# Slot numbers of a routed expert layer found for two experts at a time, in four rounds

## The chip, the cores and the metric

The kernel is one program on one core of a Trainium2 chip. The core has five engines that run their own instruction streams and meet only at semaphores: TensorE (PE, matrix products; its weight loads are listed apart as PEld), VectorE (DVE), ScalarE (ACT), GpSimd (POOL) and SyncE (SP, which issues most DMA transfers). The metric is the device time of one execution in microseconds. Smaller is better.

## What is computed

A decoder block on `x` of 2 x 1024 tokens by 256: a linear recurrence with a gate, a cross attention of 16 heads, and an expert layer, each followed by a sum with its input and a layer norm. The change lies in the expert layer, whose reference is, cut to what matters:

```python
Sm = jax.nn.softmax(xf @ Wr + br, axis=-1)     # 2048 tokens, 8 experts
G_t, idx_t = jax.lax.top_k(Sm.T, k)            # each expert takes its k = 256 tokens
tokens = xf[idx]
mid = jax.nn.silu(jnp.einsum('keh,ehf->kef', tokens, W_up[group]) + b_up[group])
out = jnp.einsum('kef,efh->keh', mid, W_down) + b_down
y = jnp.zeros_like(xf).at[idx].add(G[..., None] * out)
```

## The kernel before

Everything is written out by hand: no scheduler moves an instruction, and each engine runs its rows in the order of the code. Eight PSUM banks are handed out by a table (`product(name, bank)`): PE takes its turn on a bank with `turn(name)`, which waits until the last result there was moved away, and `wait_filled` and `wait_moved` are the waits of the others.

The expert layer begins with 15 rounds of a search for each expert's threshold (DVE and ACT count, PE adds up). Then DVE turns the chosen tokens into slot numbers 0 to 255 for each expert: prefix sums, two products for the offsets (banks 4 and 5), and the slot split in a high and a low digit of 16 values each, `sl_f` (L1960). What follows is what the change touches, the way from slots to `idx`, the token number of each slot:

- DVE compares both digits with 0 to 15 for all eight experts at once (`one_hot`, L1966). A one-hot tile is 128 partitions by 16 columns of tokens (NT) by 16 digit values by 8 experts. This is done in two halves over NT: low digit `OHL`, high digit `OHH`, then `OHT` = `OHL` times the token number (L1975). ACT spread the token numbers over `token_b` in two parts beside rounds 10 and 11 of the search (L1057).
- PE adds 16 products of `OHH` and `OHT` up in bank 6 (L1500, product "ids"). It gives 128 x 128 numbers: (high digit, expert) by (low digit, expert), of which those of the same expert count.
- DVE masks them (`ym`), sums over experts (`lk`) and multiplies by a mask of row positions (`lh`): L1980, L1983, L1984. PE makes one product with `mask_16` (L1505, "idx"), and DVE copies it out as whole numbers (`idx`, L1987).
- POOL then issues 16 indirect DMAs (L832), one for 128 rows of `XG` each. Gathers 2e and 2e+1 are the tokens of expert e. PE meanwhile makes 12 products that nobody reads (`keep_busy(0, 12)`, L1154).

Then `expert_steps` runs: "gt" transposes an expert's tokens (PE L1514 and L1520; ACT copies them to `FTH`, DVE makes the low part `FTL`), "up" is three pairs of products into banks 0, 1, 2, 7 in turn (L1544 for the first six, then L1144), with SiLU in place and `MH` by ACT (L1088, L1094 to L1097) and `ML` by DVE (L2007 to L2011), "dn" is the product with `W_down` (L1564), scaled by DVE (`OUT`, L1997) and added to DRAM by POOL (L842). Expert 0 is gt 0, up 0 and 1, gt 1, up 2. POOL issues no L842 before the sixteenth gather.

## Time and profile before

| | us |
|---|---|
| median of three runs | 317.17 |
| lowest and highest | 316.96, 317.83 |
| the profiled execution | 318.26 |
| its span | 316.1 |
| PE busy | 254.3 (80%) |
| DVE busy | 199.7 (63%) |
| ACT busy | 156.0 (49%) |
| POOL busy | 133.8 (42%) |

The span is the time from the first to the last instruction of the profiled execution. 2.16 us of that execution lie around it. The rows further down are from this execution, in microseconds from its span's start. The stretch from `sl_f` to the end of expert 0 is about 200 to 236 us. A row of the timeline gives an operation's start and length, the engine and the line, what is written and read, and in brackets how long the engine had been idle before it and what ended that. The chain of waits is followed back from the last instruction of the program, so that each piece of it is a piece of the time.

### The profile page before, as it was taken

To read this page: it belongs to the slowest core of one execution; us is meant where nothing else is said; L and a number is where in the kernel's file an instruction comes from. 1 tells how busy PE (TensorE), PEld (TensorE's weight loads), DVE (VectorE), ACT (ScalarE), POOL (GpSimd) and SP (SyncE) were. 2 spreads that over 40 slices of the span, in tenths; PEclk is the share of its full clock that TensorE was granted. 3 is DMA by queue.
4 is the path that set the end of the run, shared out by engine and by line. 5 is a ranking of instruction groups with operands and counts; after the bars stand their busy time and mean duration, and the time that the engine had idled before them with its cause. 6 is when DMAs were issued, how large, how long until landed. Compare 5 with 4: busy or idle time off the path is not lost.

```text
span 316.1 us, 5069 instructions
## 1 busy us (share of the span) xinstructions
PE 254.3 (80%) x1647; PEld 204.6 (65%) x1647; DVE 199.7 (63%) x613; ACT 156.0 (49%) x322; POOL 133.8 (42%) x211
## 2 busy tenths in 40 slices
PE   8989999899898999999963111385679999999791
PEld 4744557575556789988951101245679999999790
DVE  1744467378867578578785998810156676777394
ACT  4643312534778364744232775102147787875224
POOL 6817915525353135543232491067521333333133
PEclk9999999999999999999995555569569999999998
DMA  6960031045385638200004999123303856422646
GB/s 188 305 108 1 1 76 27 0 89 110 70 181 99 154 70 181 50 2 3 1 0 112 318 408 350 53 68 107 101 0 45 229 125 137 115 29 27 155 149 261
DMA packets 33403, 35.59 MB, mean 113 GB/s; under 512 B 10338, under 2 KB 25698, under 8 KB 33122
## 3 DMA queue, kind: packets, MB, share of 16 engines
q1 hardware_dynamic: 30002, 31.16, 35.6%
q0 software_dynamic: 2784, 4.00, 7.5%
q8 instruction: 14, 0.23, 0.3%
q10 hardware_dynamic: 592, 0.12, 0.2%
q14 instruction: 11, 0.09, 0.1%
HBM read 18.16 MB, written 8.19 MB: 83 GB/s over the span
## 4 chain that ended last, share of the span: by engine, by line
PE 56%; DVE 18%; ACT 10%; issue 4%; POOL 4%; another core or an unknown queue 4%; DMA 3%; SPq 0%; DVEq 0%; POOLq 0%; ACTq 0%
PE bank L1144 11%; PE bank L1381 8%; PE bank L1564 6%; PE bank L1332 4%; PE bank L1230 3%; DVE junk L1905 3%; PE bank L1154 3%; PE bank L1301 2%; PE bank L1368 2%; ACT bank L1088 2%; POOL rstd L778 2%; PE bank L1315 2%; DMA Y<-summed_rows 2%; PE bank L1404 1%
## 5 line engine op out<-in xcount | busy, mean ns | idle before, releaser
L777 POOL TENSOR_SCALAR var_eps<-mean_var 128x1 f32<-128x1 f32 (+2 forms) x37 | 8.4, 228 | 79.7 <-DVE mean_var L1752 79.2
L842 POOL DMA_INDIRECT summed_rows<-OUT,idx x14 | 21.7, 1550 | 44.9 <-DVE OUT L1997 42.8
L1381 PEld LDWEIGHTS bank<-VB,PT 128*128 128x128 f32 x256 | 32.4, 191 | 1.5
L1144 PE MATMUL bank<-FTH,WUH 128*128 128x256 f32 x94 | 28.0, 298 | 6.3 <-issue 6.3
L1381 PE MATMUL bank<-VB,PT 128*128 128x34 f32 x256 | 30.9, 268 | 0.0
L1088 ACT ACTIVATE bank<-bank,b_up_c 128x256 f32<-128x256 f32 (+1 forms) x48 | 19.5, 446 | 22.3 <-remote 11.0
L1564 PE MATMUL bank<-WDH,MH 128*128 128x256 f32 x80 | 24.3, 303 | 3.6 <-DVE ML L2011 3.2
L1144 PE MATMUL bank<-FTL,WUH 128*128 128x256 f32 x94 | 27.1, 289 | 0.0
L1144 PE MATMUL bank<-FTH,WUL 128*128 128x256 f32 x94 | 27.1, 288 | 0.0
L1759 DVE TENSOR_REDUCE NMF<-bank 128x8 f32<-128x512 f32 x32 | 21.7, 680 | 6.6 <-PE bank L1344 6.3
L2007 DVE TENSOR_TENSOR ML<-bank,MH 128x512 fp32r<-128x512 f32 x16 | 11.0, 688 | 20.7 <-ACT MH L1094 20.7
L778 POOL TENSOR_TENSOR rstd<-var_eps,neg_half 128x1 f32<-128x1 f32 (+2 forms) x37 | 22.7, 615 | 3.1
L832 POOL DMA_INDIRECT XG<-routed_rows,idx x16 | 15.5, 966 | 20.3 <-DVE idx L1987 15.7
L1564 PE MATMUL bank<-WDH,ML 128*128 128x256 f32 x80 | 23.4, 292 | 0.1
L1564 PE MATMUL bank<-WDL,MH 128*128 128x256 f32 x80 | 23.4, 292 | 0.0
L1144 PEld LDWEIGHTS bank<-FTH,WUH 128*128 128x128 f32 x94 | 18.8, 200 | 6.5 <-issue 6.5
L953 ACT ACTIVATE PT<-bank 128x512 f32<-128x512 f32 x32 | 18.6, 596 | 6.0 <-PE bank L1368 5.9
L1564 PEld LDWEIGHTS bank<-WDH,MH 128*128 128x128 f32 x80 | 16.1, 201 | 4.4 <-DVE ML L2011 4.0
L1144 PEld LDWEIGHTS bank<-FTL,WUH 128*128 128x128 f32 x94 | 18.9, 201 | 0.0
L1144 PEld LDWEIGHTS bank<-FTH,WUL 128*128 128x128 f32 x94 | 18.7, 199 | 0.0
L1477 PE MATMUL bank<-cnt,same_expert 128*128 128x3 bf16 x15 | 2.5, 164 | 19.4 <-DVE junk L1905 19.4
L1368 PE MATMUL bank<-QS,KS 128*128 128x512 f32 x32 | 15.2, 474 | 2.9 <-ACT QS L988 1.3
(341 smaller groups left out, 761.6 us busy)
## 6 DMA issues: line engine op xcount, KB each, us to landing
WDR<-in_L_ffn_W_down SPq DMA_DIRECT2D x8, 640.0 KB
QS<-QH SPq DMA_DIRECT2D x32, 128.0 KB, 2.6
WUR<-in_L_ffn_W_up SPq DMA_DIRECT2D x4, 682.0 KB, 5.4
routed_rows<-X SPq DMA_DIRECT2D x2, 1056.0 KB, 10.3
X<-in_x SPq DMA_DIRECT2D x4, 512.0 KB, 5.2
QS<-QL SPq DMA_DIRECT2D x16, 128.0 KB, 2.6
summed_rows<-X SPq DMA_DIRECT2D x2, 1024.0 KB, 9.7
Y<-summed_rows SPq DMA_DIRECT2D x8, 256.0 KB, 5.0
```

Of the source, the lines that this page charges most:

```text
L778: pool.tensor_tensor(rstd[:, at], var_eps[:, at], neg_half[:, 0:width], ALU.pow).then_inc(ln_pool, 1)
L832: pool.indirect_dma_start(XG[:, s, :], None, routed, bass.IndirectOffsetOnAxis(ap=idx[:, s:s + 1].bitcast(U32), axis=0)).then_inc(gathered ...
L842: pool.indirect_dma_start(summed, bass.IndirectOffsetOnAxis(ap=idx[:, 2 * e + h:2 * e + h + 1].bitcast(U32), axis=0), OUT[:, (2 * e + h) % ...
L953: act.activation(PT[m % 2][:, j, :], bank_of(("sc", m, j))[:], ACT.Exp, scale=SCALE)\
L1088: last = act.activation(mid[0:w, i], mid[0:w, i], ACT.Silu, bias=b_up_c[0:w, g, f:f + 1])
L1144: last = pe.matmul(o, a, b, start=(n == 0), stop=(n == 3 * len(pairs) - 1))
L1332: last = pe.matmul(o[:, :], WQ[:, k, c * P:(c + 1) * P], X1[n][:, k], start=(k == 0), stop=(k == KC - 1))
L1368: pe.matmul(o[:, :], KS[:, j, m // 2, :], QS[:, r, j, :], start=True, stop=True)\
L1381: last = pe.matmul(o[:, j * 34:(j + 1) * 34], PT[m % 2][:, j, s * P:(s + 1) * P], VB[:, m // 2, j].rearrange("p h d -> p (h d)"), start=Tr ...
L1564: pe.matmul(o[:, 0:D], a[:, e % 4, f, cols], b[:, e % 3, f], start=(f == 0 and k == 0), stop=False)
L1759: dve.tensor_reduce(NMF[:, t % 2, c * half:(c + 1) * half], bank_of(name)[:].rearrange("p (h k) -> p h k", k=SE), AX.X, ALU.max, negate=Tr ...
L2007: dve.tensor_tensor(ML[:, e % 4, fs], mid, MH[:, e % 4, fs].bitcast(F32), ALU.subtract)\
```

## The change

The way from `sl_f` to `idx` is cut in four rounds, each for a pair of experts (`PAIR` = 2).

- A round has one-hot tiles of 16 x 16 x 2 = 512 columns instead of 16 x 16 x 8 in two halves of 1024. Round k's 16 products are of 32 columns by 32 columns and go to banks 6, 5, 3, 4. `token_b` is one tile of 512 columns, made once.
- The three DVE operations `ym`, `lk`, `lh` become one (`by_slot`), on 32 partitions by 256 columns, with a mask `mask_place` that holds both masks. `lh` is f16, and the product for `idx` becomes two products of one pass each, one for each expert of the pair.
- POOL waits for its round before every fourth gather instead of once.
- `keep_busy(0, 12)` goes. Six of its products stand in pairs between the rounds.
- The fourth round stands inside expert 0: its one-hot tiles on DVE after gt 0, its 16 products on PE after up 1, `by_slot` on DVE after `ML` of up 1, PE's pair of products after up 2, and the copy to `idx` after `ML` of up 2.
- The one-hot tiles and `token_b` move within `MH`, and the setup of the masks changes by a few small DVE operations.

PE between the offsets and expert 0, before. `OHH`, `OHT` are the one-hot tiles, `mask_66` is `mask_16`, and `ones_b` rows are the unread products:

```order
L1495 MATMUL bank<-cig,ones_b 128x128
L1500 MATMUL bank<-OHT,OHH 128x128 [waits onehot_made,moved6]
L1500 MATMUL bank<-OHT,OHH 128x128 x7
L1500 MATMUL bank<-OHT,OHH 128x128 [waits onehot_made]
L1500 MATMUL bank<-OHT,OHH 128x128 x7
L1505 MATMUL bank<-mask_66,lh 128x16 [waits moved7,lh_made]
L1154 MATMUL bank<-ones_b 128x512 [waits moved7,moved0]
L1154 MATMUL bank<-ones_b 128x512 x11
```

The same place after (`mask_66` is `mask_4`), the first two rounds and the beginning of the third:

```order
L1506 MATMUL bank<-OHT,OHH 32x32 [waits onehot_made,moved6]
L1506 MATMUL bank<-OHT,OHH 32x32 x15
L1514 MATMUL bank<-mask_66,lh 128x4 [waits moved7,moved6]
L1514 MATMUL bank<-mask_66,lh 128x4
L1506 MATMUL bank<-OHT,OHH 32x32 [waits onehot_made,moved5]
L1506 MATMUL bank<-OHT,OHH 32x32 x15
L1159 MATMUL bank<-ones_b 128x512 [waits moved0]
L1159 MATMUL bank<-ones_b 128x512
L1514 MATMUL bank<-mask_66,lh 128x4 [waits moved7,moved5]
L1514 MATMUL bank<-mask_66,lh 128x4
L1159 MATMUL bank<-ones_b 128x512 x2
L1506 MATMUL bank<-OHT,OHH 32x32 [waits onehot_made,moved3]
```

The one long sum became three short ones with their own read-outs (the third ends below the rows shown), and the twelve unread products became two, two and two.

DVE from the first one-hot tile to `idx`, before:

```order
L1966 TENSOR_TENSOR OHL<-sl_f,digit_b 128x1024 [waits slots_made]
L1966 TENSOR_TENSOR OHH<-sl_f,digit_b 128x1024
L1975 TENSOR_TENSOR OHT<-OHL,token_b 128x1024 [waits step_made,low_digit]
L1966 TENSOR_TENSOR OHL<-sl_f,digit_b 128x1024
L1966 TENSOR_TENSOR OHH<-sl_f,digit_b 128x1024
L1975 TENSOR_TENSOR OHT<-OHL,token_b 128x1024 [waits step_made,low_digit]
L1980 TENSOR_TENSOR ym<-bank,mask_own 128x128 [waits filled6]
L1983 TENSOR_REDUCE lk<-ym 128x16 [waits moved6]
L1984 TENSOR_TENSOR lh<-lk,mask_lo_65 128x128 [waits dve_step]
L1987 CAST idx<-bank 128x16 [waits filled7]
```

and after, up to the copy of the second round:

```order
L1988 TENSOR_TENSOR OHL<-sl_f,digit_b 128x512 [waits slots_made]
L1988 TENSOR_TENSOR OHH<-sl_f,digit_b 128x512
L2000 TENSOR_TENSOR OHT<-OHL,token_b 128x512 [waits step_made,low_digit]
L1988 TENSOR_TENSOR OHL<-sl_f,digit_b 128x512
L1988 TENSOR_TENSOR OHH<-sl_f,digit_b 128x512
L2007 TENSOR_TENSOR lh<-bank,mask_place 32x8x2x16 [waits filled6]
L2000 TENSOR_TENSOR OHT<-OHL,token_b 128x512 [waits low_digit]
L2013 CAST idx<-bank 128x4 [waits filled7]
L2007 TENSOR_TENSOR lh<-bank,mask_place 32x8x2x16 [waits filled5]
L1988 TENSOR_TENSOR OHL<-sl_f,digit_b 128x512
L1988 TENSOR_TENSOR OHH<-sl_f,digit_b 128x512
L2013 CAST idx<-bank 128x4 [waits filled7]
```

The first `idx` now stands behind six tiles of 512 columns and one operation on the bank; the second round's last tile stands ahead of it, and the third round's tiles stand ahead of the second `idx`.

DVE in expert 0, from `FTL` of the first rows to the low part of the next weights, before:

```order
L2029 TENSOR_TENSOR FTL<-bank,FTH 128x2x128 [waits fth_made,stack_masks]
L2033 TENSOR_TENSOR FTL<-bank,FTH 128x2x128 [waits fth_made]
L2007 TENSOR_TENSOR ML<-bank,MH 128x512 [waits mh_made] x2
L2033 TENSOR_TENSOR FTL<-bank,FTH 128x512 [waits fth_made]
L2010 TENSOR_TENSOR ML<-bank,MH 128x256 [waits mh_made]
L2011 SCALAR_TENSOR_TENSOR ML<-bank,stack_low,MH 128x256
L2042 TENSOR_TENSOR WUL<-WUR,WUH 128x1536 [waits wu_hi]
```

and after:

```order
L2069 TENSOR_TENSOR FTL<-bank,FTH 128x2x128 [waits fth_made,stack_masks]
L2073 TENSOR_TENSOR FTL<-bank,FTH 128x2x128 [waits fth_made]
L1988 TENSOR_TENSOR OHL<-sl_f,digit_b 128x512
L1988 TENSOR_TENSOR OHH<-sl_f,digit_b 128x512
L2000 TENSOR_TENSOR OHT<-OHL,token_b 128x512 [waits low_digit]
L2047 TENSOR_TENSOR ML<-bank,MH 128x512 [waits mh_made] x2
L2007 TENSOR_TENSOR lh<-bank,mask_place 32x8x2x16 [waits filled4]
L2073 TENSOR_TENSOR FTL<-bank,FTH 128x512 [waits fth_made]
L2050 TENSOR_TENSOR ML<-bank,MH 128x256 [waits mh_made]
L2051 SCALAR_TENSOR_TENSOR ML<-bank,stack_low,MH 128x256
L2013 CAST idx<-bank 128x4 [waits filled7]
L2089 TENSOR_TENSOR WUL<-WUR,WUH 128x1536 [waits wu_hi]
```

The fourth round's three tiles come ahead of the first `ML`, its read-out between `ML` of up 1 and `FTL` of expert 1, and its `idx` behind `ML` of up 2.

The diff, without the renamed semaphores and the places of tiles:

```diff
-        product("ids", 6)
-        product("idx", 7)
+        for k in range(PAIRS):
+            product(("ids", k), (6, 5, 3, 4)[k])
+            product(("idx", k), 7)
...
             for s in range(NT):
+                if s % (2 * PAIR) == 0:
+                    wait_moved(pool, ("idx", s // (2 * PAIR)))
                 pool.indirect_dma_start(
...
-                      10: (tokens_spread, 0), 11: (tokens_spread, 1),
+                      10: (tokens_spread,),
...
+            def slot_numbers(k):
+                o = turn(("ids", k))
+                pe.wait_ge(onehot_made, k + 1)
+                for t in range(NT):
+                    last = pe.matmul(o[0:PR_ROWS, 0:PR_ROWS], OHH[:, k, t].rearrange("p s e -> p (s e)"),
+                                     OHT[:, k, t].rearrange("p s e -> p (s e)"), start=(t == 0), stop=(t == NT - 1))
+                last.then_inc(sem_filled(("ids", k)), 1)
+
+            def row_numbers(k):
+                wait_moved(pe, ("ids", k))
+                o = turn(("idx", k))
+                for i in range(PAIR):
+                    last = pe.matmul(o[:, 0:2 * PAIR], lh[:, k, i].rearrange("p a l -> p (a l)"), mask_4[0:PR_ROWS, :],
+                                     start=(i == 0), stop=(i == PAIR - 1))
+                last.then_inc(sem_filled(("idx", k)), 1)
+
+            slot_numbers(0)
+            row_numbers(0)
+            slot_numbers(1)
+            wait_moved(pe, "st")
+            keep_busy(0, 2)
+            row_numbers(1)
+            keep_busy(0, 2)
+            slot_numbers(2)
+            keep_busy(0, 2)
+            row_numbers(2)
...
-            wait_moved(pe, "st")
-            wait_moved(pe, "idx")
-            keep_busy(0, 12)
             for kind, *at in expert_steps:
                 {"gt": tokens, "up": up, "dn": down}[kind](*at)
+                if (kind, *at) == ("up", 0, 1):
+                    slot_numbers(PAIRS - 1)
+                if (kind, *at) == ("up", 0, 2):
+                    row_numbers(PAIRS - 1)
...
-                    dve.tensor_scalar(mask_16[:], col_f[:, 0:16], pf[:, 1:2], None, ALU.is_equal)
+                    dve.tensor_scalar(mask_4[:], col_f[:, 0:4], pf[:, 1:2], None, ALU.is_equal)
+                    for i in range(PAIR):
+                        dve.tensor_scalar(mask_place[:, :, i], col_f[:, 0:8], pf[:, 4:5], mask_own[:, i:i + 1],
+                                          ALU.is_equal, ALU.mult)
...
-            dve.tensor_tensor(ym[:], bank[6][:, 0:P].rearrange("p (s e) -> p s e", e=E),
-                              mask_own[:].unsqueeze(1).to_broadcast([P, 16, E]), ALU.mult).then_inc(moved[6], 1)
-            wait_moved(dve, "ids")
-            link(dve.tensor_reduce(lk[:], ym[:], AX.X, ALU.add))
-            dve.tensor_tensor(lh[:], lk[:].unsqueeze(1).to_broadcast([P, 8, 16]),
-                              mask_lo3[:].unsqueeze(2).to_broadcast([P, 8, 16]), ALU.mult).then_inc(lh_made, 1)
-            wait_filled(dve, "idx")
-            dve.tensor_copy(idx[:], bank[7][:, 0:16]).then_inc(moved[7], 1)
+            def digits(k):
+                one_hot(OHL, 1, k).then_inc(low_digit, 1)
+                one_hot(OHH, 0, k)
+
+            def by_slot(k):
+                rows = slice(0, PR_ROWS)
+                wait_filled(dve, ("ids", k))
+                got = bank_of(("ids", k))[rows, 0:PR_ROWS].rearrange("p (l e) -> p e l", e=PAIR)
+                dve.tensor_tensor(lh[:, k].rearrange("p e a l -> p a e l"), got.unsqueeze(1).to_broadcast([PR_ROWS, 8, PAIR, 16]),
+                                  mask_place[rows].unsqueeze(3).to_broadcast([PR_ROWS, 8, PAIR, 16]), ALU.mult)\
+                    .then_inc(sem_moved(("ids", k)), 1)
+
+            digits(0)
+            numbered(0)
+            digits(1)
+            by_slot(0)
+            numbered(1)
+            by_row(0)
+            by_slot(1)
+            digits(2)
+            by_row(1)
+            numbered(2)
+            by_slot(2)
+            by_row(2)
...
+                if step == ("up", 0, 0):
+                    digits(PAIRS - 1)
+                    numbered(PAIRS - 1)
                 if step[0] == "up":
                     middle_low(*step[1:])
+                    if step == ("up", 0, 1):
+                        by_slot(PAIRS - 1)
+                    if step == ("up", 0, 2):
+                        by_row(PAIRS - 1)
```

`numbered(k)` makes `OHT` of round k, and `by_row(k)` copies its four columns of `idx`.

## Rows read from the trace of the kernel before

**Rows 1.** The page: PE's granted clock and DMA share, 40 slices of 7.9 us.

```profile
PEclk9999999999999999999995555569569999999998
DMA  6960031045385638200004999123303856422646
```

**Rows 2.** The chain of waits from 200 to 236 us: start, length, what.

```profile
202.92 0.61 DVE OHT L1975
...
203.58 1.05 PE bank L1500 x8
...
205.65 0.62 PE bank L1505 x2
...
206.29 0.19 DVE idx L1987
...
206.61 4.91 PE bank L1154 x12
...
212.69 0.95 PE bank L1544 x6
...
215.82 4.49 another core or an unknown queue
...
223.07 6.47 another core or an unknown queue
...
231.70 0.40 DVE ML L2011
```

**Rows 3.** Timeline, DVE: one-hot tiles, a small 16-bit operation, 256 columns from a bank.

```profile
195.63 0.23 DVE L1945 TENSOR_TENSOR eq<-ge,gt 128x128 bf16<-128x128 bf16 x1
...
199.82 0.69 DVE L1966 TENSOR_TENSOR OHL<-sl_f,digit_b 128x1024 f16<-128x1024 f16 x1
...
212.26 0.42 DVE L2029 TENSOR_TENSOR FTL<-bank,FTH 128x256 fp32r<-128x256 f32 x1 [5.79 <-issue]
```

**Rows 4.** Timeline, PE: twelve products on 32 columns of weights; one short product alone.

```profile
165.39 0.64 PE L1415 MATMUL bank<-X2T,wr_s 128*32 128x128 f32 x12 [0.56 <-ACT X2T L1019]
...
193.16 0.16 PE L1477 MATMUL bank<-cnt,same_expert 128*128 128x3 bf16 x1 [1.24 <-DVE junk L1905]
```

**Rows 5.** Timeline, POOL: the first two gathers, the last, the first addition to DRAM.

```profile
206.78 1.26 POOL L832 DMA_INDIRECT XG<-routed_rows,idx  x1 [15.70 <-DVE idx L1987]
208.34 0.96 POOL L832 DMA_INDIRECT XG<-routed_rows,idx  x1 [0.30 <-issue]
...
225.86 0.95 POOL L832 DMA_INDIRECT XG<-routed_rows,idx  x1 [0.30 <-issue]
...
235.03 1.63 POOL L842 DMA_INDIRECT summed_rows<-OUT,idx  x1 [8.03 <-DVE OUT L1997]
```

**Rows 6.** The tile XG: the gathers' lengths in ns and their landing.

```profile
L832 POOL DMA_INDIRECT XG<-routed_rows,idx x16: 942/946/1265, 206.8 to 225.9; - x16
...
DMA to landing us min/median/max: 2.8/3.0/3.1
```

**Rows 7.** Timeline, PE and ACT in expert 0: first transposition, last product of up 1, ACT's waits.

```profile
211.36 0.38 PE L1514 MATMUL bank<-ident,XG 128*128 128x128 f32 x2
...
215.42 0.28 PE L1144 MATMUL bank<-FTH,WUL 128*128 128x256 f32 x1
...
220.33 0.81 ACT L1088 ACTIVATE bank<-bank,b_up_c 128x256 f32<-128x256 f32 x2 [4.51 <-remote]
...
229.56 0.81 ACT L1088 ACTIVATE bank<-bank,b_up_c 128x256 f32<-128x256 f32 x2 [6.49 <-remote]
```

**Rows 8.** Busy time by stretch: PE, PEld, DVE, ACT, POOL, granted clock, DMA share, GB/s.

```profile
140.00:150.00 10.00, 9.66 (x94) 9.13 (x93) 8.25 (x34) 4.49 (x11) 3.62 (x7) 1.00 0.01 2
...
217.60:223.80 6.20, 0.00 (x0) 0.00 (x0) 1.38 (x2) 2.00 (x4) 4.68 (x6) 0.79 0.38 107
```

**Rows 9.** The same columns, two stretches at the lower clock.

```profile
207.60:211.00 3.40, 3.40 (x10) 1.22 (x8) 0.00 (x0) 0.00 (x0) 2.49 (x4) 0.50 0.30 80
...
224.70:228.10 3.40, 3.40 (x18) 3.40 (x18) 0.00 (x0) 0.00 (x0) 2.00 (x3) 0.50 0.41 117
```

More of the change, by code:

```diff
@@ L110, in decoder_block @@
         mask_lo3 = place("mask_lo3", [P, 8], F32)
-        mask_16 = place("mask_16", [P, 16], F32)
+        mask_4 = place("mask_4", [P, 4], F16)
         steps = place("steps", [P, ROUNDS, 8], F32)
@@ L228, in decoder_block @@
         ML = place("ML", [P, 4, FC, TOP], F32R)
-        OHH = place("OHH", [P, NT, 16, E], F16, offset_of["MH"])
-        OHL = place("OHL", [P, NT, 16, E], F16, end_of["OHH"])
-        OHT = place("OHT", [P, NT, 16, E], F16, end_of["OHL"])
-        token_b = place("token_b", [P, NT, P], F16, end_of["OHT"])
+        OHH = place("OHH", [P, PAIRS, NT, 16, PAIR], F16, offset_of["MH"] + 2 * FC * TOP * 4)
+        OHL = place("OHL", [P, PAIRS, NT, 16, PAIR], F16, end_of["OHH"])
+        OHT = place("OHT", [P, PAIRS, NT, 16, PAIR], F16, end_of["OHL"])
+        token_b = place("token_b", [P, NT, PR_ROWS], F16, offset_of["MH"] + FC * TOP * 4)
+        assert end_of["OHT"] <= end_of["MH"]
         WUR = place("WUR", [P, 2, KC, FP], F32)
@@ L827, in _ @@
             down_low(1)
-            wait_moved(pool, "idx")
+            wait_moved(pool, ("idx", 0))
             pool.wait_ge(routed_out, 16 * B)
@@ L1053, in up_high, with tokens_spread @@
                         last.then_inc(wu_hi, 1)
-            def tokens_spread(part):
-                at = slice(part * NT // 2, (part + 1) * NT // 2)
-                act.activation(token_b[:, at], token_f[:, at].unsqueeze(2).to_broadcast([P, NT // 2, P]), ACT.Copy)\
+            def tokens_spread():
+                act.activation(token_b[:], token_f[:].unsqueeze(2).to_broadcast([P, NT, PR_ROWS]), ACT.Copy)\
                     .then_inc(step_made, 1)
@@ L1495, in _ @@
             pe.matmul(o[:, 0:P], ones_b[:], rows_g, start=False, stop=True).then_inc(filled[5], 1)
-            o = turn("ids")
-            for t in range(NT):
-                if t % (NT // 2) == 0:
-                    pe.wait_ge(onehot_made, 2 * t // NT + 1)
-                last = pe.matmul(o[:, 0:P], OHH[:, t].rearrange("p s e -> p (s e)"),
-                                 OHT[:, t].rearrange("p s e -> p (s e)"), start=(t == 0), stop=(t == NT - 1))
-            last.then_inc(filled[6], 1)
-            pe.wait_ge(lh_made, 1)
-            o = turn("idx")
-            pe.matmul(o[:, 0:16], lh[:].rearrange("p a l -> p (a l)"), mask_16[:], start=True, stop=True)\
-                .then_inc(filled[7], 1)
+            def slot_numbers(k):
[22 more added lines that the diff above has]
+            row_numbers(2)
             def tokens(e):
@@ new lines, in numbered @@
+            def numbered(k):
+                dve.wait_ge(low_digit, k + 1)
+                if k == 0:
+                    dve.wait_ge(step_made, 1)
+                dve.tensor_tensor(OHT[:, k].rearrange("p t s e -> p (t s e)"), OHL[:, k].rearrange("p t s e -> p (t s e)"),
+                                  token_b[:].rearrange("p t s -> p (t s)"), ALU.mult).then_inc(onehot_made, 1)
+            def by_slot(k):
[5 more added lines that the diff above has]
+                    .then_inc(sem_moved(("ids", k)), 1)
@@ new lines, in by_row @@
+            def by_row(k):
+                wait_filled(dve, ("idx", k))
+                dve.tensor_copy(idx[:, 2 * PAIR * k:2 * PAIR * (k + 1)], bank_of(("idx", k))[:, 0:2 * PAIR])\
+                    .then_inc(sem_moved(("idx", k)), 1)
+            digits(0)
[9 more added lines that the diff above has]
+            by_slot(2)
```

49 lines of the change are left out of this document (20 added, 29 removed).

## The prediction

> **What bounds the kernel now.** I read the chain of waits first [rows 2]. Between 200 and 206.5 us it is the way from slots to `idx`: the last one-hot tile on DVE at 202.92, the second eight products on PE at 203.58, three short DVE operations, a product pair at 205.65, the copy at 206.29. In all this time POOL is idle: its first gather starts at 206.78 after 15.7 us of idle time that this copy ends [rows 5]. Then comes the unread work, 4.91 us in twelve products, which ends at 211.52. The first transposition starts at 211.36 [rows 7]. The first gather lands at about 209.8 (206.78 + 3.0, [rows 6]) and the second, which gt 0 needs too, at 208.34 + 3.0 = 211.3, so the unread products and the second gather end together: both must come earlier if expert 0 is to start earlier. It starts its products at 212.69.
>
> The largest pieces behind that are no work at all: 4.49 us from 215.82 and 6.47 us from 223.07, in which ACT waits for a signal that the profile gives to an unknown queue [rows 2]. ACT's operations there wait for PE's up 1 and up 2 [rows 7], and PE's last product of up 1 starts at 215.42, some 4.6 us before ACT goes on. PE is idle from 217.6 to 223.8 for want of what ACT makes next [rows 8]. These 11 us, which I call the hold, lie inside the stretch of gathers (206.78 to 228.9). The trace does not say what makes it, and that is the main uncertainty here. The clock view [rows 1] shows PE at its lower level (1.2 GHz) through the search, and at 207.6 to 211.0 it is still at 0.50 [rows 9].
>
> **The change part by part.** First to `idx`. The DMA view is near empty from 198 us on [rows 1], so the rows in DRAM that POOL also waits for are there. DVE's tiles shrink from 1024 columns to 512. A 16-bit operation of 128 columns takes 0.23 us and one of 1024 takes 0.69 [rows 3], so by the line through both 512 take 0.43, and two in a row start 0.34 apart where they were 0.61 apart [rows 2, 3]. `OHT` of round 0 ends at 199.82 + 0.34 + 0.34 + 0.43 = 200.93. If the runs of two experts instead of eight cost the faster pace, the two comparisons keep 0.60 each: 0.5 later.
>
> PE's 16 products of 32 columns do not stand in the trace. Eight of 128 columns take 1.05 at the lower clock [rows 2]; twelve with 32 columns of weights and 128 of data take 0.64 at the full one, 0.053 each, and one short product alone is done in 0.16 [rows 4]. Lower bound 16 x 0.053 + 0.16 = 1.0, upper bound 2 x 1.05 = 2.1. I take 1.1, near the first, since that row has the same width of weights: 202.1. `by_slot` is 256 columns from a bank, 0.42 [rows 3]: 202.5. The product behind it takes 0.62 now, with f32 operands in two passes [rows 2]; in f16 it is at least one short product's 0.16 [rows 4], and I take 0.3 for the pair: 202.9. The copy ends 0.2 later and POOL starts 0.3 after that, as it does now (206.29 to 206.78): 203.4. The gathers start **3.4 us earlier**; bounds, with 0.5, 1.0 and 0.3 lost, 1.6, and with everything at its least, 3.7.
>
> Then PE's own line to expert 0. Round 1: products 202.95 to 204.05, two unread ones of 4.91 / 12 = 0.41 each, a pair 0.3: 205.2. Two unread: 206.0. Round 2: 1.1, 0.8, 0.3: 208.2. DVE's `by_slot` of each round fits behind the unread products that follow (0.42 against 0.82). So expert 0's first transposition can start at 208.2 against 211.36, and the second gather lands at 203.4 + 1.56 + 3.0 = 208.0. Expert 0 starts **3.1 us earlier**, at 209.6. Here the upper bound of PE's sums counts three times (3.0) and that of the pairs twice more: then nothing is gained; the other end is 3.7. What queues behind the new waits: POOL's gathers 4 to 15. Round 1's `idx` is there at 205.4, gather 4 is due at 203.4 + 1.56 + 3 x 1.25 = 208.7 (1.25 apart as the last 14 of now, [rows 5]), and round 2's (208.4) is due at 213.7. Rounds 1 and 2 cost POOL nothing.
>
> Inside expert 0 work is added. Three tiles on DVE (1.1 us) stand ahead of the first `ML`, which waits for ACT's 1.4 us of SiLU and copy, so they hide. PE's 16 products (1.1 us, half of it at the full clock) stand ahead of gt 1. And the clock: the twelve unread products fill PE at 207.6 to 211.0 without a gap (3.40 of 3.40, [rows 9]), and expert 0 runs at the full level. After the change PE has gaps in every round, so I expect expert 0 to start at the lower one, where a product costs 3.40 / 18 = 0.19 [rows 9], against (215.42 - 212.69) / 23 = 0.12 now [rows 2, 7]. For the 24 products of up 0 and up 1 that is up to 1.7 us, less if the level comes back within them. Both additions, 2.8 us, go into PE's 6.2 us of idle time [rows 8] as long as the hold lasts: that cover is what I count on, and without it they are on the path.
>
> The fourth `idx` is made only behind `ML` of up 2 (232.1 now, [rows 2]), while gather 12 is due about 218.8. POOL waits there for some 10 us, then needs 5.0 us for four gathers, and its first addition to DRAM, now at 235.03 with 8.0 us of idle time ahead of it [rows 5], comes 2 to 3 us late. Nobody waits for it before expert 2's `OUT`, two experts later: nothing on the path. The masks add about four small DVE operations of at most 0.23 each near 144 to 148, where PE is busy 9.66 of 10 us and DVE 8.25 [rows 8]: taken as nothing, at most 0.9. One of ACT's two spreads goes, but a search round ends with DVE's count, not ACT's [rows 4]: nothing.
>
> The third and fourth rounds' DVE tiles now run beside POOL's gathers, which no DVE tile of two SBUF inputs does in this trace (the gathers' lengths are 942 to 946 ns but for the first, [rows 6]). At worst they hold POOL up for their own 2.1 us; half of that could touch the second gather, 1.0 us on the path. The Trainium skill (SBUF — State Buffer, Who interferes with whom) speaks against the change here: a DVE instruction with two SBUF inputs shares its second read port with GpSimd, and whoever comes second is blocked for the whole instruction; but it adds, as inferred, that descriptor generation needs the write side. By its first sentence the sum would be 1.0 worse; no row here shows it.
>
> **Sum**, against the profiled execution's 318.26: less 3.1 for expert 0's start, nothing for the rest while the hold stays as long after that start as now, gives 315.2. The runs' median is 1.1 below that execution: **314.1 us**.
>
> **The rivals.** (1) *The hold ends with the gathers.* It ends at 229.5, and the last gather lands at 225.86 + 3.0 = 228.9. After the change the gathers break off after the twelfth, which starts at 203.4 + 1.56 + 10 x 1.25 = 217.5 and lands at 220.5. ACT would go on near 221.2 instead of 229.56. Then PE's own work bounds: from 209.6 it has up 0 and 1 (24 products), the sum (1.1), gt 1, up 2, up of expert 1 and 18 products of dn 0, some 66 at 0.12 to 0.19, plus waits for ACT, 223 to 225.5 against 232.1. That gives 7 to 9 us: 308 to 310. For it: all late signals lie among gathers. Against: the gathers run since 206.78 [rows 5], and the chain has no such piece before 215.82 [rows 2]. That the hold vanishes altogether gives about the same, 307 to 309. (2) *The hold is counted from PE's last signal.* PE is through with up 2 before its idle time, at about 217.5, and ACT goes on 12 us later. With 3.1 gained, 1.1 lost to the fourth sum, and up to 2.8 lost at the lower clock (40 products and transpositions, 0.07 each), up 2 ends 0.8 us later than now, or 1.8 with the collision of tiles and gathers: 318.0 to 319.0. This is the slower side: the fourth round's sum ahead of gt 1 together with the lower clock, decisive if the clock stays down through up 2. (3) *The rounds are not shorter*: PE's short products cost what the wide ones do (2.1 a round, 0.6 a pair), three rounds reach 211, and the time is 316.2 to 317.2. A part of it gives 315 to 316.
>
> **Numbers.** The forecast 0.38 (313 to 315.2), the rivals: hold ends with the gathers or vanishes 0.28, rounds partly longer 0.07, not shorter 0.12, hold counted from PE's signals or something else that lengthens expert 0 0.15. A measurement of this kernel tells about 0.3% (1 us) from no change. Faster by more: 0.38 + 0.28 + 0.07 = 0.73. Within: 0.12. Slower by more: 0.15. The range goes from 307.0 to 318.4 us; below lies a hold that vanishes with nothing else in its place, above a longer hold.
>
> **What would show it.** Right: POOL's first gather near 203.4 and expert 0's first transposition near 208.2, each round's 16 products in 1.0 to 1.2 us, POOL waiting for the fourth `idx` with no one waiting for POOL, an unknown queue of about 11 us still in the chain, the clock low at expert 0's start. Wrong: the unknown queue shorter with its end after the twelfth gather (rival 1); ACT's release in up 2 at 229.5 or later (2); a first transposition near 211 (3); DVE or PE waiting for POOL.

## The result, and the profile after

The kernel after the change takes 314.09 us in the median of six executions, the kernel before 317.83 us in its six beside it. The ratio is 0.9869, with a 95% interval of 0.9835 to 0.9904: some 4.2 us less, 3.1 to 5.2. The profiled execution of the changed kernel was one of its two slow ones (319.19 us, its span 317.4; both stand in the median of 314.09 and neither in the ratio, and the other four have a median of 313.1) and lost some 6 us in the attention part, where the clock fell for 13.7 us. So positions are counted below from the start of the first one-hot tile, which is at 199.82 before and at 205.82 after.

The page after the change, granted clock and DMA share, 40 slices of 7.9 us; it answers to [rows 1]:

```profile
PEclk9999999999997589999999755567769999999998
DMA  6950031034374605520000799814123856422647
```

The chain of waits after the change from 206 to 236 us: start, length, what. It answers to [rows 2]:

```profile
207.06 0.60 PE bank L1506 x16
...
207.69 0.41 DVE lh L2007
...
208.43 0.14 DVE idx L2013
...
208.64 0.86 issue
209.50 1.27 POOL XG L838
...
211.07 2.75 DMA XG<-routed_rows,idx
...
215.24 1.56 PE bank L1564 x6
...
219.56 2.02 another core or an unknown queue
...
223.05 3.65 another core or an unknown queue
...
229.74 0.08 DVE idx L2013
229.82 0.14 issue
229.95 2.90 PE bank L1149 x12
232.85 3.86 PE bank L1584 x21
```

The first part went as planned: the first gather starts 3.68 us behind the first tile (6.96 before), and expert 0's first products 9.42 us behind it (212.69 - 199.82 = 12.87 before). The second part did not. The unknown queue has 2.02 + 3.65 = 5.67 us of the chain, not 11.65. What it gave up is not in the time, and the chain says what took its place: expert 1's first products (229.95) now follow a DVE copy to `idx`, and run in 2.90 and 3.86 us for 12 and 21 products.

Timeline after the change, PE, POOL and DVE. In brackets the idle time before the operation and what ended it; it answers to [rows 5] and [rows 7]:

```profile
229.95 0.55 PE L1149 MATMUL bank<-FTH,WUH 128*128 128x256 f32 x1 [2.61 <-DVE idx L2013]
...
223.67 0.95 POOL L838 DMA_INDIRECT XG<-routed_rows,idx  x1 [0.31 <-issue]
230.07 2.22 POOL L838 DMA_INDIRECT XG<-routed_rows,idx  x1 [5.46 <-DVE idx L2013]
...
229.72 1.75 DVE L2089 TENSOR_TENSOR WUL<-WUR,WUH 128x1536 fp32r<-128x1536 f32 x1
```

PE waits 2.61 us for that copy. `FTL`, which PE waited for at this place before, is ready at 228.04, so 1.9 of the 2.61 us are the copy's. The fourth round's row numbers stand in bank 7, and expert 1's first pair of `up` is the next to use bank 7 (`UP_BANKS`), so these products may not start before DVE has copied `idx` out; and DVE does that behind `ML` of up 2. The prediction had POOL waiting there and nobody else.

Positions behind the first one-hot tile, in us. "Expert 2's rows" is the first transposition of gt 2 as the chain of waits has it (the timeline's row starts 0.16 to 0.20 earlier), the end of the stretch in which both kernels differ. All of it is from one trace each.

| kernel | first gather | expert 0 starts | expert 1 starts | expert 2's rows | end of span |
|---|---|---|---|---|---|
| before | 6.96 | 12.87 | 24.03 | 35.68 | 116.3 |
| after | 3.68 | 9.42 | 24.13 | 32.21 | 111.6 |

So 3.4 us are won up to expert 0, the same 3.5 stand at expert 2's rows, and 1.2 more come behind them.

### The profile page after: what moved, and what is told of

It reads as the page before. It is cut to its first block, busy times and chain, and to the rows that moved or that the text cites. A ratio compares the mean times of both kernels' runs of the same rounds, so it can differ in the third digit from the quotient of the medians.

```text
span 317.4 us, 5181 instructions
## 1 busy us (share of the span) xinstructions
PE 258.0 (81%) x1695; PEld 208.7 (66%) x1695; DVE 202.0 (64%) x625; ACT 155.0 (49%) x321; POOL 135.4 (43%) x211
## 4 chain that ended last, share of the span: by engine, by line
PE 58%; DVE 16%; ACT 10%; issue 5%; POOL 4%; DMA 4%; another core or an unknown queue 2%; SPq 1%; DVEq 0%; POOLq 0%; ACTq 0%
PE bank L1149 12%; PE bank L1386 9%; PE bank L1584 6%; PE bank L1337 5%; PE bank L1235 3%; DVE junk L1928 3%; PE bank L1373 2%; PE bank L1306 2%; ACT bank L1093 2%; POOL rstd L782 2%; DMA Y<-summed_rows 2%; PE bank L1320 2%; PE bank L1349 1%; PE bank L1409 1%
## 5 line engine op out<-in xcount | busy, mean ns | idle before, releaser
L848 POOL DMA_INDIRECT summed_rows<-OUT,idx x14 | 21.7, 1551 | 36.9 <-DVE OUT L2037 34.8
L1386 PEld LDWEIGHTS bank<-VB,PT 128*128 128x128 f32 x256 | 35.1, 205 | 1.8
L1386 PE MATMUL bank<-VB,PT 128*128 128x34 f32 x256 | 33.3, 279 | 0.0
L1782 DVE TENSOR_REDUCE NMF<-bank 128x8 f32<-128x512 f32 x32 | 21.7, 680 | 9.4 <-PE bank L1349 9.2
L838 POOL DMA_INDIRECT XG<-routed_rows,idx x16 | 16.8, 1052 | 22.1 <-DVE idx L2013 17.9
L782 POOL TENSOR_TENSOR rstd<-var_eps,neg_half 128x1 f32<-128x1 f32 (+2 forms) x37 | 22.8, 616 | 3.1
L1337 PE MATMUL bank<-X,WQ 128*128 128x512 f32 x32 | 17.4, 669 | 1.5 <-ACT X L974 1.5
L1373 PE MATMUL bank<-QS,KS 128*128 128x512 f32 x32 | 16.2, 507 | 2.9 <-ACT QS L994 1.3
```

What stands on the lines that cost most here:

```text
L782: pool.tensor_tensor(rstd[:, at], var_eps[:, at], neg_half[:, 0:width], ALU.pow).then_inc(ln_pool, 1)
L838: pool.indirect_dma_start(XG[:, s, :], None, routed, bass.IndirectOffsetOnAxis(ap=idx[:, s:s + 1].bitcast(U32), axis=0)).then_inc(gathered ...
L848: pool.indirect_dma_start(summed, bass.IndirectOffsetOnAxis(ap=idx[:, 2 * e + h:2 * e + h + 1].bitcast(U32), axis=0), OUT[:, (2 * e + h) % ...
L1337: last = pe.matmul(o[:, :], WQ[:, k, c * P:(c + 1) * P], X1[n][:, k], start=(k == 0), stop=(k == KC - 1))
L1373: pe.matmul(o[:, :], KS[:, j, m // 2, :], QS[:, r, j, :], start=True, stop=True)\
L1386: last = pe.matmul(o[:, j * 34:(j + 1) * 34], PT[m % 2][:, j, s * P:(s + 1) * P], VB[:, m // 2, j].rearrange("p h d -> p (h d)"), start=Tr ...
```

## Experiments

Each kernel ran beside the kernel before on the same chip; every ratio is to that. The first eleven ran on three chips where the kernel before takes 306 to 307 us and no late signal stands in any chain. The twelfth fell on one where it takes 316.99.

**A pause of the gathers, in both kernels.** `e1_pause`, and the same two lines in the kernel before for `e4_before_pause`:

```diff
...
             for s in range(NT):
...
+                if s == 4:
+                    wait_filled(pool, ("up", 0, 2))
```

> The changed kernel with one wait more: POOL waits for PE's last product of up 2 of expert 0 before gather 4. Only four gathers then run beside the start of expert 0, the other twelve start behind it. Theory A (the late signals of PE go with the gathers; they ended at 226.64 to 226.82, as the twelfth gather, which started at 223.67, landed): with no gather in flight from about 216.6 on, ACT goes on at once behind up 1 and up 2, the unknown queue of 5.7 us leaves the chain, and expert 1 comes some 4 us earlier: 308 to 310 us against about 313.1 for the changed kernel. Theory B (the hold comes from something in expert 0 itself, or is counted from PE's last signal): nothing but the gathers moves, the unknown queue stays at 5 to 6 us, 313 to 314; if gathers 4 and 5 come too late for expert 2, above that.

> The kernel before with one wait more: POOL waits for PE's last product of up 2 of expert 0 before gather 4. Here the chain has 4.49, 0.69 and 6.47 us of an unknown queue, 11.65 in all, which ends at 229.54, 0.7 us after the sixteenth gather lands. Theory A (the signals go with the gathers): four gathers are in by about 214, the 11.65 us shrink to under 2, part comes back at a lower clock and as PE's own work: 308 to 311 us against 317.4. Theory B (something else in expert 0): the unknown queue stays and the time is 317 to 318 or more.

Measured: 1.0031 (1.0005 to 1.0057) and 0.9999 (0.9980 to 1.0018); the kernel before took 306.68 us. Neither theory was tested: with or without a pause there was nothing to remove. What follows is another thing: the same kernel before is 10 to 12 us shorter on a chip without the late signals, about the 11.65 us of its chain [rows 2]. And a pause of the gathers costs the kernel before nothing there.

**The unread products.** `e2_no_unread` leaves out `keep_busy(0, 2)` three times in the changed kernel; `e3_before_no_unread` leaves out `keep_busy(0, 12)` in the kernel before.

> The changed kernel without its three pairs of unread products. Theory A (the second gather's landing sets the start of expert 0; the changed kernel's PE waits 0.67 us for it with the unread products in): the start of expert 0 does not move, 313.1 within 0.5. Theory B (the unread products bring the clock level up for expert 0's first products): the granted clock stays at 0.50 through expert 0's first 24 products, 0.07 us each, up to 1.7 us later, 313.5 to 315. Theory C (they are on the path): up to 1 us faster.

> The kernel before without its twelve unread products ahead of expert 0. The second gather lands at about 211.3, the unread products end at 211.5. Theory A: the start of expert 0 stays within 0.3 us, and whatever the clock takes in expert 0 goes into PE's idle time while ACT waits for PE's late signals: 316.5 to 317.8. Theory B: without them the clock stays low for expert 0 and that is on the path: 318 to 319.5. Part of the gain of the change would then be an effect of the clock alone.

Measured: 1.0089 (1.0056 to 1.0122) and 1.0059 (1.0035 to 1.0082). The second is theory B: twelve products that nobody reads are worth 1.8 us. The mean granted clock of its executions is 0.908 to 0.912, that of the kernel before beside them 0.915 to 0.921. The chain of waits of `e3_before_no_unread` in expert 0, and below it that of the kernel before with a pause (`e4_before_pause`), which keeps the twelve:

```profile
212.78 1.62 PE bank L1544 x6
214.40 3.85 PE bank L1144 x18
218.25 0.02 issue
```

```profile
212.91 0.96 PE bank L1546 x6
213.86 0.71 PE bank L1146 x6
214.58 0.02 issue
214.60 0.82 ACT bank L1090 x2
```

Both start expert 0 at the same place (212.8, 212.9). Without the unread products its first 24 take 5.47 us at the lower level (1.2 GHz); with them the first 12 take 1.67 at the higher (2.4 GHz). `e2_no_unread` stands 0.24% above the changed kernel's 1.0065 below, inside the intervals of both: it is not told from it, and none of its three theories is shown. Nor do the traces settle it. The first 24 products take 4.6 us without the six unread products (`e2_no_unread`), and with them 5.46 (`e1_pause`), 4.6 (the first trace) and 2.98 (`k5_after`): six of them, broken up by waits, don't set the level.

**Both kernels on one chip, the placement of the fourth round, and more unread products.** `k5_after` and `k6_before` are the two kernels as they are. `k7_ten_unread`:

```diff
...
-            keep_busy(0, 2)
+            keep_busy(0, 3)
             row_numbers(1)
-            keep_busy(0, 2)
+            keep_busy(0, 3)
             slot_numbers(2)
-            keep_busy(0, 2)
+            keep_busy(0, 4)
             row_numbers(2)
```

`k8_fourth_ahead` (DVE's and PE's steps of that round go behind the third, and leave `expert_steps`):

```diff
...
             row_numbers(2)
+            slot_numbers(3)
+            row_numbers(3)
...
-                if (kind, *at) == ("up", 0, 1):
-                    slot_numbers(PAIRS - 1)
-                if (kind, *at) == ("up", 0, 2):
-                    row_numbers(PAIRS - 1)
```

> The changed kernel itself, beside the kernel before on the same chip. On the chip of the last four runs the kernel before took 306.68 us, not 317, and the unknown queue stood in no chain. Theory A (where PE's signals are not late, the 3.4 us won on the way to the first gather are given back in expert 0 at the lower clock: with the pause of the gathers, its first 24 products took 5.46 us at the lower clock where the kernel before needs 1.67 for the first 12 at the higher): where the kernel before takes 306.7, this takes 307 to 308.5, and the unknown queue is in neither trace. Theory B (the gain does not depend on the late signals): 302 to 304 where before takes 306.7. If this chip is like the first one (before at 317), A and B both give 313 to 314.

> The kernel before itself, for its trace on this chip. Theory A: where it takes about 306.7, its chain from 200 to 236 us has no piece of an unknown queue, expert 0 and 1 follow each other as PE's own work, and the span is 11 us shorter than the 316.1 of the rows on record, about what the three pieces of the unknown queue added up to (11.65), less what lower clock or ACT take back. Where it takes 317, the three pieces are there again.

> The changed kernel with 3, 3 and 4 unread products in its rounds instead of 2, 2 and 2: ten in all, 1.6 us more of PE's time ahead of expert 0, in a stretch in which PE waited some 0.7 us for the second gather and for DVE. Theory A (the clock level in expert 0 is what the shorter rounds lost, and PE's filled time brings it up): expert 0's first 24 products go from 5.4 us towards 2.9, its start moves by at most 1.0 us, and the time is 1 to 2 us below the changed kernel's. Theory B (the level does not follow from unread products broken up by waits): the start is up to 1.0 us later at the same level, so the time is 0.5 to 1.0 above the changed kernel's.

> The changed kernel with its fourth round ahead of expert 0, behind the third, and not inside it. DVE's tiles of 0.41 us stand ahead of FTL, PE's 16 products and the pair (0.8 us, and a wait for DVE's 0.41) ahead of the first transposition, which so starts at about the time of the second gather's landing or up to 1.5 us behind it. POOL no longer waits ahead of gather 12. Theory A (inside expert 0 the fourth round is paid on PE's and DVE's line where nothing holds them up, 0.5 to 1.1 us; ahead of it, part of it hides behind the second gather): the same as the changed kernel within 1 us where the signals are not late. Where they are late, and go with the gathers, the gathers run without a break to the sixteenth, and it is 3 to 5 us slower than the changed kernel. Theory B (the hold doesn't go with the gathers): within 1 us of the changed kernel there too.

Measured, the kernel before at 305.93 us: the changed kernel 1.0065 (1.0039 to 1.0091), ten unread products 1.0014 (0.9990 to 1.0038), the fourth round ahead 0.9990 (0.9967 to 1.0014). The chain of `k6_before` has no piece of the unknown queue, and from the first tile to the end it is 12.8 us shorter than before (103.5 against 116.3), the 11.65 us and a little of the lower clock. On this chip the change makes the kernel 2 us **slower**: theory A of `k5_after`, though not by the cause that it names. Its trace has the higher clock in expert 0. PE in the timeline of `k6_before` and then of `k5_after`, expert 1's first product:

```profile
224.06 0.39 PE L1144 MATMUL bank<-FTH,WUH 128*128 128x256 f32 x1 [1.00 <-DVE FTL L2033]
```

```profile
217.83 0.35 PE L1149 MATMUL bank<-FTH,WUH 128*128 128x256 f32 x1 [2.50 <-DVE idx L2013]
```

Busy time of PE by stretch in `k5_after`: stretch, its length, PE, granted clock, DMA share, GB/s:

```profile
214.00:216.00 2.00, 1.24 (x11) 1.00 0.28 82
216.00:218.00 2.00, 0.17 (x1) 1.00 0.50 135
218.00:220.00 2.00, 2.00 (x11) 0.54 0.27 68
220.00:222.00 2.00, 2.00 (x13) 0.61 0.25 68
222.00:224.00 2.00, 2.00 (x19) 1.00 0.54 141
```

The wait for the copy to `idx` is 1.5 us longer than the wait for `FTL` was. PE stands nearly still from 215.4 to 217.8, the granted clock is 0.54 and 0.61 in the four microseconds behind that, and 12 + 21 products take 2.63 + 3.03 us where `k6_before` has 1.65 + 2.50. Together 3.0 us of the 3.9 that are lost between expert 0's start and expert 2's rows; the fourth round's 16 products (0.49) come to it.

The clock does not fall behind every such wait. PE in the timeline of `e1_pause`, the same product, and its chain from there:

```profile
221.25 0.36 PE L1151 MATMUL bank<-FTH,WUH 128*128 128x256 f32 x1 [2.52 <-DVE idx L2015]
```

```profile
221.25 1.61 PE bank L1151 x12
222.86 2.50 PE bank L1586 x21
```

The wait is as long, and the 33 products run at the higher level. There expert 0 had begun at the lower one, and the level came up 2.7 us ahead of the wait. So the 1.5 us of the wait come with the bank, and the 1.5 us of the clock in some traces (`k5_after`, `k7_ten_unread`, `e2_no_unread`) and not in all. The positions:

| kernel | first gather | expert 0 starts | expert 1 starts | expert 2's rows | end of span |
|---|---|---|---|---|---|
| `k6_before` | 6.95 | 12.57 | 18.41 | 23.89 | 103.5 |
| `k5_after` | 3.67 | 9.19 | 17.45 | 24.44 | 104.4 |
| `k8_fourth_ahead` | 3.68 | 9.91 | 18.23 | 23.70 | 103.2 |

3.4 us ahead at expert 0, 0.55 behind at expert 2's rows. `k8_fourth_ahead` starts expert 0 0.7 us later and is 0.75% faster, because nothing of the fourth round stands in expert 0 then: its 33 products take 1.65 + 2.50 us again. Its expectation spoke of 1 us and knew nothing of the bank. `k7_ten_unread` is 0.5% faster than the change. Its profiled run doesn't show where (24.81 at expert 2's rows, one trace against one); over its executions the mean granted clock is 0.915 to 0.929 against 0.906 to 0.919. That is theory A by the clock, not by a trace of expert 0.

**The bank alone, and combinations.** `k9_bank`:

```diff
...
-            product(("idx", k), 7)
+            product(("idx", k), 7 if k < PAIRS - 1 else 4)
```

`k10_bank_ten` has this line and the unread products of `k7_ten_unread`. `k11_ahead_ten` is `k8_fourth_ahead` with 3, 3, 2 and 2 unread products (the last two between the fourth round's 16 products and its pair) and `numbered(3)` ahead of `by_row(2)` on DVE.

> The changed kernel with one number changed: the fourth round's row numbers go into bank 4, where that round's slot numbers stand, and no longer into bank 7, which the first products of expert 1 need next. In the changed kernel's trace PE is idle for 2.50 us ahead of those products and goes on when DVE has copied the fourth idx out of bank 7, where in the kernel before PE waits 1.00 us for FTL; then the products and the 21 behind them run at the lower clock for 3.5 us. Theory A (that bank is what the change lost inside expert 0): PE goes on with FTL, some 2.1 us earlier, and most of the lower clock behind it (1.5 us) goes too: 2 to 3.5 us below the changed kernel, 0.992 to 0.998 of the kernel before where that takes 306; where PE's signals are late it also lets expert 1's first products go into the wait: 0.975 to 0.98 there. Theory B (PE waits for the next thing at once, DVE's FTL and ML of up 2 or the clock): within 0.7 us of the changed kernel, 1.004 to 1.009 of the kernel before.

> Both: row numbers of the fourth round in bank 4, and 3, 3 and 4 unread products in the rounds. The ten unread products alone gave 306.26 against 308.26 for the changed kernel (1.0014 and 1.0065 of the kernel before). Theory A (the bank and the clock at the start of expert 0 are two separate losses): 3.5 to 5 us below the changed kernel, 0.985 to 0.993 of the kernel before. Theory B (what the unread products gave was the clock behind the same idle time of PE, so the two don't add): the same as the bank alone within 0.7 us.

> The changed kernel with the fourth round ahead of expert 0, now with 3, 3, 2 and 2 unread products, and DVE's third OHT tile ahead of the third idx. Without that the fourth round ahead gave 305.86 (0.999 of the kernel before), with expert 0's first 24 products at the lower clock in the profiled run (1.62 + 3.85 us against 0.94 + 2.04). Theory A (filled time brings the clock up for expert 0): they take 3.0 us at the higher clock, the start of expert 0 moves by 0.5 to 1.5 us, 0.5 to 1.5 us below that: 0.994 to 0.998. Theory B (the start moves more than the clock gives): 0.998 to 1.003.

Measured, the kernel before again at 305.93 us: the bank alone 0.9948 (0.9916 to 0.9980), bank and ten products 0.9935 (0.9911 to 0.9959), ahead with ten 0.9953 (0.9932 to 0.9974). One number changed takes 1.2% off the changed kernel (two chips, on both of which the kernel before takes 305.93) and puts it below the kernel before: theory A. PE in the timeline of `k9_bank`:

```profile
219.19 0.39 PE L1149 MATMUL bank<-FTH,WUH 128*128 128x256 f32 x1 [0.32 <-DVE FTL L2073]
```

PE waits for `FTL` again, and 33 products behind it take 1.65 + 2.50 us as in the kernel before, even though expert 0 ran at the lower level in this trace (its first 24 products 1.62 + 3.85 us). The time does depend on that level: four executions with a mean clock of 0.920 to 0.927 take 302.1 to 303.7 us, five with 0.911 to 0.916 take 305.6 to 306.2. With the fourth round ahead, filled rounds give 0.37% on `k8_fourth_ahead`, in the range of theory A of `k11_ahead_ten` (the two intervals overlap a little; in its trace expert 0 does run at the higher level and starts 0.5 us later), and the kernel comes out even with the bank alone. Ten unread products on top of it give 0.13% more, less than can be told: theory B of `k10_bank_ten` by the number, but not by its cause. PE did gain by both: expert 0 and expert 1 run at the higher level, and expert 2's rows come 1.9 us earlier than in the trace of `k9_bank` (21.7 against 23.6). Its trace says what took that back. The chain of waits of `k10_bank_ten`, from the last gather on, and one DVE row of its timeline:

```profile
224.78 1.64 POOL summed_rows L848
226.41 0.30 issue
226.72 6.43 DMA summed_rows<-OUT,idx
233.15 0.27 issue
233.41 1.55 POOL summed_rows L848
234.97 0.30 issue
235.27 6.39 DMA summed_rows<-OUT,idx
```

```profile
220.54 0.48 DVE L2037 TENSOR_SCALAR OUT<-bank,XG 128x256 f32<-128x256 f32 x1
```

It reaches expert 2's rows 21.7 us behind the first tile, 2.2 ahead of `k6_before`, but its span ends only 0.9 ahead (102.6 against 103.5). Seven pairs of additions to DRAM follow each other on POOL, each pair waiting for the one before it to land, and the first waits 3.8 us behind its `OUT` for the gathers.

**The first addition ahead of the last four gathers**, on `k10_bank_ten`:

```diff
...
+            gather(range(NT - 4))
             for e in range(E - 1):
+                if e == 1:
+                    gather(range(NT - 4, NT))
+                    pool.tensor_copy(own_row[:], idx[:, NT - 2:NT]).then_inc(rows_ready, 1)
                 if e:
                     pool.wait_ge(scattered[e - 1], 32)
```

> The kernel with ten unread products and the fourth row numbers in bank 4 (0.9935 of the kernel before), with POOL's order changed: gathers 12 to 15, for experts 6 and 7, stand behind expert 0's two additions to DRAM, not ahead. In its trace the chain no longer runs through PE from 209 to 281 us but through POOL: the last gather ends at 224.40, the first addition starts at 224.78 though its OUT was made at 221.0, and each later one starts as the one before it has landed (6.4 to 7.0 us). Theory A (POOL's additions are the next bound): the first starts some 3.5 us earlier, the four gathers fit into the 4.8 us in which POOL waits for its landing, and the end comes 1 to 3 us earlier: 0.983 to 0.990 of the kernel before. Theory B (the two lines, PE's and POOL's, are even, so PE's own work bounds at once, or the additions slow down beside the gathers): the same within 0.7 us, 0.991 to 0.996. On a chip where PE's signals are late, both are lower, since the kernel before takes some 317 there.

Measured: 312.76 us against 316.99, 0.9869 (0.9822 to 0.9916). This chip has the late signals, so the question of the additions stays open: POOL's first addition (230.86) waits 11.9 us for `OUT` here. But the run shows the late signals a third time, with gathers that end earlier. Its chain of waits:

```profile
209.71 4.13 another core or an unknown queue
...
215.30 4.94 another core or an unknown queue
220.24 0.02 issue
...
223.40 2.93 PE bank L1153 x12
226.34 3.60 PE bank L1588 x21
```

The DMA share from 205 to 235 us in 40 slices of 0.75 us, of the kernel before, of the changed one and of this one (each run's own view; these are the packets of the gathers):

```profile
DMA  0000054251543516325164251532506000000000
```

```profile
DMA  1000000032625435063341623516000000000515
```

```profile
DMA  1432617425162351614510000000000001000672
```

The first unbroken stretch of gathers is over at 228.3, 226.0 and 220.8. The last of ACT's waits for a late signal ends at 229.54, 226.69 and 220.24. Twice the stretch was cut by four gathers, and both times the late signals ended with it. In two of the three traces the four gathers come back later (changed kernel at 230.07, this one at 234.67), and ACT's waits for PE are short there:

```profile
232.89 0.81 ACT L1093 ACTIVATE bank<-bank,b_up_c 128x256 f32<-128x256 f32 x2 [4.00 <-PE bank L1149]
```

That one is given to PE, whose last product of the group starts at 232.44. So gathers in flight are not enough for late signals, and on the other chips the same sixteen gathers make none. That they end with the stretch is read from three traces; no run moved the gathers alone on such a chip. In this run, too, PE goes on right behind `FTL` (0.32 us of idle time at 223.40), since the fourth row numbers are in bank 4.

## Why the prediction was right, point by point

**The number is right, by luck; the account of expert 0 is not.** The forecast was 3.1 us off the profiled execution, 314.1; measured were 314.09 and a ratio that stands for 4.2 us. What a shorter hold gave, which the sum didn't have, went into a wait that it didn't have either and into PE's own work behind the hold. That the two figures agree to 0.01 says nothing.

- *The way to `idx`*: right in sum. First gather 3.58 us behind the first tile forecast, 3.68 measured, in all traces of the changed rounds 3.67 to 3.69. Two terms were off and cancelled. The 16 short products take 0.60 us, not 1.1, and less than the lower bound of 1.0: I took a pace of 0.053 from products of 128 columns of data, and these have 32. In return POOL starts 1.10 us behind the start of the copy to `idx` (208.40 to 209.50), not 0.49 as in [rows 5]. What those 0.6 us are no run tells; the thirteenth gather starts 0.41 behind the start of its copy (229.66 to 230.07).
- *Expert 0's start*: forecast 3.1 us earlier, 3.45 measured. The second gather's landing sets it: PE waits 0.67 us for it.
- *The hold stays as long*: wrong. It went from 11.65 to 5.67 us, with its end at the twelfth gather's landing, as rival 1 said (forecast 221.2 in the time of before, measured 226.69 - 6.0 = 220.7). Rival 1 had 0.28 and put the time at 308 to 310. (The 4.6 us that the prediction counts from the start of PE's last product to ACT are counted from its end, 215.70; from its start it is 4.9.)
- *Both additions inside expert 0 hide in PE's idle time*: right while there is a hold. Behind up 2 PE is still idle for 4.56 us, up to 227.13.
- *Nobody on the path waits for the fourth `idx`*: wrong, and this is the step that failed. The sum looked at who reads `idx` (POOL) and not at who needs its bank next. PE waited 2.61 us for the copy. In the kernel before, expert 1's first products and a part of dn 0 lay inside the hold (PE starts them at 223.85, six microseconds before ACT goes on); they ran at the lower clock there, too, but at no cost. After the change they stand behind the hold. That took back what the shorter hold gave: from expert 0's start to expert 2's rows it is 22.8 us before and 22.8 after. Without a hold the wait for the bank and the lower clock make the change 0.65% slower (`k5_after`), and the bank alone is 1.2% (`k9_bank`).
- *The lower clock at expert 0's start*: in the changed kernel's trace the first 24 products take 4.6 us (215.24 to 219.83) against 3.0 before, 1.6 of the 1.7 allowed. The allowance was small: 0.19 a product comes from 18 records in 3.40 us [rows 9], some of which only reach into that stretch, while the starts there are 0.21 apart. With all 24 at the lower level they take 5.47 us against 2.98 (`e3_before_no_unread`, `k6_before`), 2.5 more. That it costs nothing holds only beside a hold; without one the twelve unread products are worth 1.8 us (`e3_before_no_unread`).
- *POOL's wait*: 5.46 us, not 10, and its first addition is not late (31.8 us behind the first tile, 35.2 before). Without a hold the additions are the next bound (`k10_bank_ten`).
- *DVE tiles beside gathers*: the one-hot tiles cost next to nothing, but not because they leave the gathers alone. A gather that began at 216.09, beside an `OHT` tile of 215.88 to 216.30, took 1.02 us, not 0.95, and ended at 217.11. The gather at 230.07 began inside the subtraction for `WUL` (229.72 to 231.47), took 2.22 and ended at 232.29. Both end 0.81 to 0.82 us behind the end of the DVE operation. So do the gathers that begin inside the `WUL` operation in eleven other traces (0.81 to 0.83, with lengths of 1.36 to 2.52 us). Beside `ML`, `FTL` and `OUT`, which take one input from a bank, gathers keep 0.94 to 0.95, but for one of 1.02 (`k12_first_sum_earlier`, 234.67). So a gather that begins inside a DVE operation with both inputs in SBUF is held until that operation ends, in the 16-bit tiles of 512 columns as in the f32 operation of 1536. The Trainium skill (SBUF — State Buffer, Who interferes with whom) has the port rule and infers that a `tensor_tensor` leaves descriptor generation alone; the rule agrees with both rows, and neither shows an indirect DMA that goes free. Whether its read of `idx` is held or the making of its descriptors no run tells. The tiles are short, and so is what they hold up: 0.07 us here, at most 0.24 in the other traces (1.19 us for a gather in `k10_bank_ten`), not the 1.0 that the prediction allowed.
- *Masks*: the first tile starts at 199.57 to 201.07 us in eight traces with the new masks, mean 200.4, and at 199.82 to 200.05 in three without (three that lost 5 to 6 us ahead of it left out). Some 0.4 us, inside the bound.

What stays open is what makes PE's signals late on two of the five sets of runs, and so where 10 to 12 us of this kernel go there. The experiment for it, a pause of the gathers after the fourth, ran twice, on a chip that has no such signals.

## What to carry to other kernels

When a small product is moved into a busy stretch, follow its bank to the next user as well as its result to its reader: a wait for a bank that a slow consumer clears can cost more than the product (1.5 us against 0.5 here), and in three traces the clock fell behind it, which cost as much again (1.5 us in `k5_after`); in `e1_pause` it did not. When a big piece of the chain has no cause that the profile shows, forecast for a chip with it and for one without; the same edit was 1.3% faster with it and 0.65% slower without. After such an edit, change one bank number before giving the idea up: here it turned the loss into 0.5% of gain.

## What the runs showed of the chip

- The same kernel takes 306 to 307 us on some chips and 317 on others, and by one trace of each the difference is the three late signals in expert 0: PE's last product of up 1 starts at 215.42, ACT goes on at 220.33 [rows 7], with nothing in the profile between.
- Sixteen products of 32 by 32 columns take 0.59 to 0.60 us at the granted clock of 0.50 and 0.49 to 0.51 at 1.0: they hardly depend on the clock, where products of 256 columns take 0.21 and 0.12.
- After 2.4 us of nearly idle PE in `k5_after` the granted clock was 0.54 and 0.61 in the next four microseconds: the longer wait cost 1.5 us of its own and 1.5 more in the 33 products behind. After the same wait in `e1_pause`, where the level had come up only 2.7 us before it, it stayed at 1.00.
- An indirect DMA that POOL begins while DVE works on two inputs from SBUF waits for DVE's end: gathers (0.95 us) end 0.81 to 0.84 us behind it, and additions to DRAM of 128 rows (1.54 us) mostly 1.42 behind it. In `k10_bank_ten` the addition at 226.72 took 1.86 us, beside the `WDL` subtraction of 225.68 to 227.16; the one at 261.41, where a second such operation follows at once, took 3.52.
